# A decoder layer on one core: the attending stage with its instruction and bank orders laid out anew

## The chip, the cores and the metric

The kernel runs on one core of a Trainium2 chip. The metric is device time in microseconds (us), as the median of several runs. A core has a matmul engine (TensorE, PE in the profile; its weight loads are PEld), VectorE (DVE), ScalarE (ACT), GpSimd (POOL) and SyncE (SP), which here only issues DMAs. Each engine works through its own list of instructions in order; semaphores tie the lists together.

## The reference

For 8 sequences of 512 tokens and 512 features, in f32, three blocks follow one another, each with a residual and a layer norm behind it:

```python
x = _layernorm(x + _L0_attn_ref(x, w_qkv, w_out))        # Fourier mixing, a cumulative sum over tokens
x = _layernorm(x + _L0_xattn_ref(x, ctx, ctx, mask, ...)) # 16 heads, 77 keys for each sequence
x = _layernorm(x + _L0_ffn_ref(x, kernel, bias, a, b))    # one matmul with a quantised weight plus LoRA, bias
```

The second block is q = x W_q + b_q, masked softmax(q k^T / sqrt(32)) v for each head, then W_o and b_o. The third has a single 512 x 512 weight once quantised kernel and LoRA product are added up.

## The kernel before

Three parts run one after the other: `prepare` (weights, keys, values), `mix_tokens` (the first block for all 8 sequences, whose result x1 goes to DRAM), and `attend` (the second and third block), which the change is about. A number that is an f32 is split in two, a high part (a copy to f32r) and a low part (the difference), and each product is made of three matmuls (`split_matmuls`, L85).

`attend` is a software pipeline over i. Step i does three things for three different sequences: the front (scores, softmax and transposed probabilities of sequence i), the back (weighted values, W_o, norm, feed-forward and norm of sequence i-1) and the next (the query projection of sequence i+1). Step 0 has no back, step 7 (the closing step) no next, and step 8 (the tail) only a back. Steps 1 to 6 have the same order (the loop, `step(i)` on each engine). The order of every engine's instructions is written out by hand, one call after another.

The pieces, with the engine that does each, tiles t of 128 tokens, halves h of the heads, chunks c, groups g:

- PE: `score(i,t,h)` fills half h of score_ps; `turn_probs(i,t,c)` transposes probabilities (uses P00 to P32 of a bank, L1158); `weigh_values(g)` (V0 to V3); `project_o(t)` (O0 to O3); `turn_x2(t)` transposes the normalised tile (T0 to T3, L1191); `project_f(t)` (F0 to F3); `project_q(c)` (Q0 to Q3).
- DVE: `softmax_top(t,h)` is a masking copy (L1678) and a maximum (L1683); `invert_totals(t)` a reciprocal (L1690); `split_...` the low part of what PE left in a bank (L1634, L1643, L1662), which frees the bank; `add_o`, `add_f` add the residual and free the bank (L1702); `measure(use)` is bn_stats, bn_aggr and a small add (L1708 to L1713); `normalize_o`, `normalize_f` apply mean and rstd (L1724); `turn_x1` transposes the next x1 in blocks (L1639).
- ACT: `exponentials(t,h)` are 8 exponentials with their sums (L1357); `split_...` the high parts.
- POOL: `normalize_probs(t,h)` multiplies half a tile's probabilities with the reciprocals (L1505); `root(use)` is (var + eps)^-0.5 of 128 x 1 (L1498); `bias_residual(t)`, `bias_x2(t)` add biases (L1512, L1528); `rem_x1(c)` is the low part of the next x1 (L1519).
- SP: for each step the load of x1 for i+1 in swapped blocks, its mask, the values of i, the keys of i+1, the residual of i, and the four stores of i-1 in between, each of which waits for its `normalize_f`.

All of PE's uses but the scores share a ring of four PSUM banks. The use at place n of `BANK_ORDER` (in the first, closing and last step `START_ORDER`, `CLOSING_ORDER`, `END_ORDER`) takes bank n mod 4 and waits until the use at n-4 is freed:

```python
    def reusable(self, use):
        return self.before + (self.order.index(use) + 1 - RING)
```

`freed` is one counter, so DVE must free the banks in that same order: the order of the banks ties PE's and DVE's lists together. Other waits that matter here: `turn_probs(i,t,0)` waits for both `normalize_probs` of tile t; `turn_x2(t)` for `normalize_o(t)`; `project_f(t)` for both halves of the split of turn_x2(t); `score(i,t,h)` for the exponentials of (t-1,h); `invert_totals(t)` for the exponentials of both halves of t; `split_q(c)`, `split_o(g)` and the like on DVE for ACT's high part.

Of the kernel before, what the change touches and what calls it, by code (L numbers as in the profile page):

```python
# [463 lines left out]
def mix_tokens(nc, x, x1_dram, k_dram, mask_dram, ident, sigma, w_spec, w_back, half_power, w_q_dram, w_q, bias_q, hand):  # L464
# [4 lines left out]
    with ExitStack() as ctx:  # L469
# [296 lines left out]
        def _(dve):  # L766
# [124 lines left out]
            def split_q(c):  # L891
# [25 lines left out]
BANK_ORDER = ["V0", "V1", "V2", "V3", "O0", "O1", "T0", "O2", "F0", "P00", "P01", "T1", "P02", "O3",  # L917
              "F1", "T2", "P10", "P11", "P12", "F2", "Q0", "Q1", "P20", "T3", "Q2", "P21", "P22", "F3",
# [61 lines left out]
def attend(nc, ins, out, x1_dram, k_dram, v_dram, ffn_dram, ident, half_power, w_q, bias_q, bias_v, bias_o, bias_f,  # L980
# [3 lines left out]
    with ExitStack() as ctx:  # L984
# [140 lines left out]
        def _(pe):  # L1125
# [81 lines left out]
            def step(i):  # L1207
# [46 lines left out]
            score(0, s, 1, 1)  # L1254
            turn_probs(0, s, 0, 0)
            turn_probs(0, s, 0, 1)
            score(0, s, 2, 0)
# [7 lines left out]
            project_q(1, s, 0)  # L1265
            turn_probs(0, s, 2, 0)
            project_q(1, s, 1)
            turn_probs(0, s, 2, 1)
            project_q(1, s, 2)
            turn_probs(0, s, 2, 2)  # L1270
            turn_probs(0, s, 3, 0)
            turn_probs(0, s, 3, 1)
            turn_probs(0, s, 3, 2)
# [7 lines left out]
            weigh_values(B - 2, s, 1)  # L1281
            score(B - 1, s, 1, 0)
            weigh_values(B - 2, s, 2)
            score(B - 1, s, 1, 1)
            weigh_values(B - 2, s, 3)
            score(B - 1, s, 2, 0)
# [3 lines left out]
            project_o(B - 1, s, 0)  # L1290
            project_o(B - 1, s, 1)
            score(B - 1, s, 2, 1)
            score(B - 1, s, 3, 0)
            turn_x2(B - 1, s, 0)
            project_o(B - 1, s, 2)
            turn_probs(B - 1, s, 1, 0)
            project_f(B - 1, s, 0)
            turn_probs(B - 1, s, 1, 1)
            score(B - 1, s, 3, 1)
            turn_probs(B - 1, s, 1, 2)  # L1300
# [712 lines left out]
```

## Time and profile before

| | |
|---|---|
| median of 3 runs | 946.08 us (945.35 to 946.32) |
| the profiled execution | 946.56 us, of which its span is 944.70 us |
| busy in the span | PE 890.7, PEld 729.5, DVE 675.1, ACT 378.1, POOL 414.4 us |
| attending stage | from about 465.5 us of the span to its end |

In the profile an engine is busy while an instruction of its own runs; waits on semaphores are not busy time, and a wait is put down to the engine that released it last. Ends of matmuls are modelled: they overlap, so the distance between starts is the time one takes. PEclk is the granted clock of the matmul engine as a share of 2.4 GHz.

### The profile page before, as it was taken

The page shows a single profiled execution, that of the slowest core. Times are in us where ns is not written, and L with a number is a line of the kernel's source. Part 1 is how long each engine was busy: PE and PEld are TensorE (multiplying, and loading weights), DVE is VectorE, ACT ScalarE, POOL GpSimd, SP SyncE. Part 2 cuts the span into 40 slices and gives each one's busy share as a digit, 9 for nine tenths or more (in the row PEclk, how much of TensorE's full clock was granted, in tenths as well). Part 3 has the DMA queues.
Part 4 walks back from the last instruction along what each step waited for, and adds up shares of the span by engine and source line. Part 5 has one row for each costly group of instructions (what it writes and reads, how often), then busy time and mean ns, then how long its engine had stood idle before and what let it go on. Part 6 is the DMA issues. An engine that isn't in the chain of part 4 may idle for free. (4 is left out here: it accounts for less than half of the span.)

```text
span 944.7 us, 14374 instructions
## 1 busy us (share of the span) xinstructions
PE 890.7 (94%) x4220; PEld 729.5 (77%) x4220; DVE 675.1 (71%) x1136; ACT 378.1 (40%) x1403; POOL 414.4 (44%) x366
## 2 busy tenths in 40 slices
PE   4897999999999999999779999999999999999995
PEld 4783787888888888887667888888888888888774
DVE  2364456666666676656776988888888888888957
ACT  3262221112020202102188565756557575567610
POOL 2000364433333435323356654736547364465534
PEclk9996999999999999999969999999999999999999
DMA  5965450416133320205354024151331514112021
GB/s 183 316 168 87 92 89 23 112 37 97 52 83 69 64 89 0 90 14 128 83 135 105 14 81 88 26 132 25 99 53 24 135 31 116 27 43 70 15 79 44
DMA packets 195994, 76.02 MB, mean 80 GB/s; under 512 B 170407, under 2 KB 172711, under 8 KB 195951
## 3 DMA queue, kind: packets, MB, share of 16 engines
q1 hardware_dynamic: 195951, 75.49, 32.9%
q8 instruction: 21, 0.34, 0.1%
q14 instruction: 22, 0.18, 0.1%
HBM read 52.60 MB, written 22.87 MB: 80 GB/s over the span
## 5 line engine op out<-in xcount | busy, mean ns | idle before, releaser
L1357 ACT ACTIVATE probs<-score_ps,top_s 128x77 f32<-128x77 f32 x512 | 158.8, 358 | 32.4 <-DVE top_s L1683 24.6
L1505 POOL TENSOR_TENSOR probs<-probs,per_total 128x616 f32<-128x616 f32 x64 | 84.8, 1329 | 95.7 <-DVE per_total L1690 95.2
L1357 ACT ACTIVATION_READ_ACCUMULATOR probs<-score_ps,top_s 128x1 f32 x512 | 121.7, 240 | 0.0
L703 POOL TENSOR_TENSOR xT_lo<-x_tok,xT_hi 128x512 fp32r<-128x512 f32 x28 | 37.9, 1358 | 76.9 <-ACT xT_hi L653 76.9
L719 POOL TENSOR_TENSOR vals<-qs_prod 128x512 f32<-128x512 f32 x32 | 41.0, 1293 | 69.4 <-DVE qs_prod L814 69.4
L710 POOL TENSOR_TENSOR mix_rstd<-mix_ve,half_power 128x1 f32<-128x1 f32 x32 | 22.0, 689 | 112.7 <-DVE mix_ve L833 112.6
L666 ACT ACTIVATE qT_hi<-vals 128x512 fp32r<-128x512 f32 x32 | 19.4, 631 | 122.2 <-POOL vals L719 106.4
L1498 POOL TENSOR_TENSOR rstd<-ve,half_power 128x1 f32<-128x1 f32 x64 | 37.9, 591 | 68.8 <-DVE ve L1713 68.6
L1364 ACT ACTIVATE pT_hi<-shared_ps 103x512 fp32r<-103x512 f32 (+1 forms) x96 | 53.5, 608 | 35.9 <-PE shared_ps L1158 35.8
L1678 DVE COPY_PREDICATED score_ps<-hidden,masked 128x616 f32<-128x616 int32 x64 | 58.4, 912 | 9.3 <-PE score_ps L85 8.6
L659 ACT ACTIVATE v_sb<-v_ps 128x512 f32<-128x512 f32 x32 | 18.9, 594 | 114.5 <-PE v_ps L85 114.5
L1662 DVE TENSOR_TENSOR pT_lo<-shared_ps,pT_hi 103x512 fp32r<-103x512 f32 (+1 forms) x96 | 62.6, 680 | 0.0
L85 PE MATMUL v_ps<-xT_hi,w_spec_hi 128*128 128x512 f32 x128 | 51.8, 405 | 6.6 <-DVE xT_lo L776 6.6
L1158 PE MATMUL shared_ps<-ident,probs 128*103 128x128 f32 (+1 forms) x384 | 54.5, 283 | 2.7 <-POOL probs L1505 2.7
L1512 POOL TENSOR_TENSOR x_tok<-x_tok,bias_o 128x512 f32<-128x512 f32 x32 | 46.0, 1458 | 21.4 <-DMA x_tok<-x_between 21.2
L85 PE MATMUL shared_ps<-w_o_hi,xT_hi 128*128 128x512 f32 x128 | 52.8, 413 | 2.0 <-DVE xT_lo L1643 1.8
L1158 PEld LDWEIGHTS shared_ps<-ident,probs 128*103 128x103 f32 (+1 forms) x384 | 47.9, 162 | 8.2 <-POOL probs L1505 3.4
L1683 DVE TENSOR_REDUCE top_s<-score_ps 128x8 f32<-128x616 f32 x64 | 51.2, 800 | 3.6
L85 PE MATMUL shared_ps<-w_ffn_hi,xT_hi 128*128 128x512 f32 x120 | 48.8, 407 | 4.6 <-DVE xT_lo L1634 2.9
L1519 POOL TENSOR_TENSOR xT_lo<-x,xT_hi 128x512 fp32r<-128x512 f32 x28 | 41.8, 1515 | 24.8 <-ACT xT_hi L1340 24.8
L786 DVE TENSOR_TENSOR kv_prod<-k_ps,v_sb 128x512 f32<-128x512 f32 x16 | 11.0, 685 | 57.7 <-PE k_ps L85 57.7
L85 PE MATMUL score_ps<-xT_hi,qT_hi 128*128 128x308 f32 x128 | 42.7, 334 | 9.7 <-ACT probs L1357 7.7
(205 smaller groups left out, 2723.6 us busy)
## 6 DMA issues: line engine op xcount, KB each, us to landing
x_tok<-in_x SPq DMA_DIRECT2D x32, 256.0 KB, 4.6
x_res<-in_x SPq DMA_DIRECT2D x8, 1024.0 KB, 7.0
x_between<-mix_x SPq DMA_DIRECT2D x32, 256.0 KB, 2.0
x<-x_between SPq DMA_DIRECT2D x32, 256.0 KB, 4.1
x_tok<-x_between SPq DMA_DIRECT2D x8, 1024.0 KB, 5.8
out<-y_out SPq DMA_DIRECT2D x32, 256.0 KB, 2.2
wqkv_sb<-in_w_qkv SPq DMA_DIRECT2D x4, 768.0 KB, 7.6
keys_split<-w_q_hi SPq DMA_DIRECT2D x8, 154.0 KB, 5.8
```

The costliest lines, as they stand in the source:

```text
L85: last = nc.tensor.matmul(out, l, r, start=(n == 0), stop=(n == len(terms) - 1))
L703: nc.gpsimd.tensor_tensor(xT[half][1][:, c, :], x_tok[half][:, c, :], xT[half][0][:, c, :].bitcast(F32), ALU.subtract).then_inc(x_lo, 1)
L719: nc.gpsimd.tensor_tensor(vals[:, h, :], qs[:, 2 * h, :], qs[:, 2 * h + 1, :], ALU.subtract if h else ALU.add).then_inc(vals_summed, 1)
L1158: last = nc.tensor.transpose(shared_ps[s.bank(use)][0:size, g * P:(g + 1) * P], probs[:, t % 2, g * GK + at:g * GK + at + size], ident[:])
L1357: nc.scalar.activation(probs[:, t % 2, j * KEYS:(j + 1) * KEYS], score_ps[:, g, k * KEYS:(k + 1) * KEYS], ACT.Exp, bias=top[:, t % 2, j:j ...
L1364: nc.scalar.activation(pT[0][0:size, c, :, t * P:(t + 1) * P], turned_bank(s, t, c), ACT.Copy).then_inc(turned_hi, 1)
L1505: nc.gpsimd.tensor_tensor(p, p, per_total[:, t % 2, h * heads:(h + 1) * heads].unsqueeze(2) .to_broadcast([P, heads, KEYS]), ALU.mult).the ...
L1512: nc.gpsimd.tensor_tensor(res1[:, t, :], res1[:, t, :], bias_o[:], ALU.add).then_inc(res1_ready, 1)
L1519: nc.gpsimd.tensor_tensor(x1T[1][:, c, :], x1[:, c, :], x1T[0][:, c, :].bitcast(F32), ALU.subtract).then_inc(x1T_lo, 1)
L1662: nc.vector.tensor_tensor(pT[1][0:size, c, :, tok], turned_bank(s, t, c), pT[0][0:size, c, :, tok].bitcast(F32), ALU.subtract).then_inc(fr ...
L1678: nc.vector.copy_predicated(s4, hidden[:, t, :].unsqueeze(1).unsqueeze(1).to_broadcast(shape), masked[:].unsqueeze(1).unsqueeze(1).to_broa ...
L1683: nc.vector.tensor_reduce(top[:, t % 2, h * 8:(h + 1) * 8].rearrange("p (g j) -> p g j", j=GH), s4, AX.X, ALU.max, negate=True).then_inc(t ...
```

## The change

No instruction is added, removed or altered, and no wait has another condition. Only places change: in the bank orders of the loop, first and closing step, and in the lists of PE, ACT, POOL and DVE for the loop, the first step, the closing step and (POOL and DVE only) the tail. `END_ORDER`, PE's and ACT's lists of the tail and SP's list stay. The core of the diff:

```diff
-BANK_ORDER = ["V0", "V1", "V2", "V3", "O0", "O1", "T0", "O2", "F0", "P00", "P01", "T1", "P02", "O3",
-              "F1", "T2", "P10", "P11", "P12", "F2", "Q0", "Q1", "P20", "T3", "Q2", "P21", "P22", "F3",
+BANK_ORDER = ["V0", "V1", "V2", "V3", "O0", "O1", "P00", "P01", "T0", "O2", "F0", "T1", "P02", "O3",
+              "F1", "T2", "P10", "P11", "P12", "F2", "Q0", "T3", "Q1", "P20", "Q2", "P21", "P22", "F3",
               "P30", "P31", "P32", "Q3"]
-START_ORDER = ["P00", "P01", "P02", "P10", "P11", "P12", "Q0", "P20", "Q1", "P21", "Q2", "P22", "P30",
-               "P31", "P32", "Q3"]
-CLOSING_ORDER = ["V0", "V1", "V2", "V3", "P00", "P01", "P02", "O0", "O1", "T0", "O2", "P10", "F0",
-                 "P11", "P12", "T1", "O3", "F1", "P20", "T2", "P21", "P22", "F2", "T3", "P30", "P31",
+START_ORDER = ["P00", "P01", "P02", "P10", "P11", "P12", "Q0", "Q1", "P20", "P21", "P22", "P30", "P31",
+               "Q2", "P32", "Q3"]
+CLOSING_ORDER = ["V0", "V1", "V2", "V3", "O0", "P00", "P01", "P02", "O1", "T0", "O2", "P10", "P11",
+                 "F0", "T1", "P12", "O3", "F1", "T2", "P20", "P21", "P22", "F2", "T3", "P30", "P31",
                  "P32", "F3"]
```

PE's list in the loop step:

```diff
                 score(i, s, 2, 0)
+                turn_probs(i, s, 0, 0)
+                turn_probs(i, s, 0, 1)
                 turn_x2(i, s, 0)
                 project_o(i, s, 2)
                 project_f(i, s, 0)
-                turn_probs(i, s, 0, 0)
-                turn_probs(i, s, 0, 1)
                 score(i, s, 2, 1)
...
                 turn_probs(i, s, 1, 0)
+                turn_probs(i, s, 1, 1)
                 score(i, s, 3, 1)
-                turn_probs(i, s, 1, 1)
                 turn_probs(i, s, 1, 2)
                 project_f(i, s, 2)
                 project_q(i + 1, s, 0)
+                turn_x2(i, s, 3)
                 project_q(i + 1, s, 1)
                 turn_probs(i, s, 2, 0)
-                turn_x2(i, s, 3)
```

The loop step's lists on POOL and DVE, as they are after the change, up to the parts that the prediction steps through:

```python
# POOL
bias_residual(0), bias_residual(1), normalize_probs(0,0), normalize_probs(0,1), root O0, root O1,
bias_residual(2), bias_x2(0), normalize_probs(1,0), bias_residual(3), normalize_probs(1,1), bias_x2(1),
root O2, root F0, rem_x1(0..3), root O3, normalize_probs(2,0), bias_x2(2), normalize_probs(2,1), ...
# DVE
softmax_top(0,0), split_o(0), softmax_top(0,1), split_o(1..3), softmax_top(1,0), softmax_top(1,1),
invert_totals(0), add_o(0), turn_x1(0), measure O0, add_o(1), normalize_o(0), measure O1,
split_probs(0,0), split_probs(0,1), split_x2(0), softmax_top(2,0), invert_totals(1), turn_x1(1),
add_o(2), normalize_o(1), measure O2, softmax_top(2,1), add_f(0), split_x2(1), measure F0, ...,
normalize_o(3), measure F1, softmax_top(3,1), add_f(2), split_q(0), measure F2, normalize_f(1),
invert_totals(3), ..., normalize_f(2), split_q(3), normalize_f(3)
```

Before, POOL had root O0 between the two products of tile 0 and root O1 behind bias_x2(0); DVE had invert_totals(0) ahead of softmax_top(1,1), softmax_top(2,1) behind split_x2(1), and softmax_top(3,1) ahead of normalize_o(3).

The first step, where ScalarE and VectorE now do the last half of the softmax ahead of the query splits:

```diff
             exponentials(0, 3, 0)
+            exponentials(0, 3, 1)
             split_q(1, s, 0)
+            split_q(1, s, 1)
             split_probs(0, s, 2, 0)
-            exponentials(0, 3, 1)
-            split_q(1, s, 1)
```

The tail on DVE:

```diff
             measure(B, s, "O0")
+            add_o(B, s, 1)
             normalize_o(B, s, 0)
-            add_o(B, s, 1)
             measure(B, s, "O1")
+            add_o(B, s, 2)
             normalize_o(B, s, 1)
-            add_o(B, s, 2)
+            split_x2(B, s, 0)
             measure(B, s, "O2")
-            split_x2(B, s, 0)
             add_o(B, s, 3)
...
             measure(B, s, "F0")
+            split_x2(B, s, 2)
             normalize_o(B, s, 3)
             normalize_f(B, s, 0)
-            split_x2(B, s, 2)
```

On POOL the tail now has bias_residual(0), (1), (2), root O0, bias_residual(3), bias_x2(0), root O1, bias_x2(1), root O2; before, bias_residual(2) stood behind root O0 and bias_residual(3) behind root O1.

## Rows read from the trace of the kernel before

**Rows 1.** Windows by stage: length, busy us (instructions) of each engine, granted clock, DMA.
```profile
465.50:508.70 43.20, 30.81 (x145) 26.98 (x146) 31.82 (x47) 34.03 (x150) 22.46 (x16) 0.80 0.41 93
...
565.60:851.45 285.85, 282.40 (x1461) 237.63 (x1460) 245.14 (x446) 178.19 (x780) 157.74 (x140) 1.00 0.30 69
851.45:895.77 44.32, 42.56 (x233) 35.95 (x232) 38.20 (x68) 30.96 (x149) 25.60 (x21) 1.00 0.13 38
895.77:944.70 48.93, 37.74 (x160) 29.54 (x160) 32.00 (x64) 5.74 (x10) 17.57 (x19) 0.96 0.17 59
```

**Rows 2.** Chain of waits in a loop step (i = 5): start, us, what.
```profile
753.82 0.71 DVE x L1639
...
754.63 1.34 DVE x_and_res L1724
...
762.28 0.87 PE shared_ps L1158 x8
```

**Rows 3.** Timeline of PE, same step: start, us, instruction, [idle before, releaser].
```profile
755.14 0.30 PE L85 MATMUL score_ps<-xT_lo,qT_hi 128*128 128x308 f32 x1
756.09 0.65 PE L1191 MATMUL shared_ps<-ident,x_and_res 128*128 128x128 f32 x4 [0.65 <-DVE x_and_res L1724]
...
767.88 0.40 PE L85 MATMUL shared_ps<-w_ffn_hi,xT_hi 128*128 128x512 f32 x1
```

**Rows 4.** Timeline of POOL, same step.
```profile
750.63 1.59 POOL L1505 TENSOR_TENSOR probs<-probs,per_total 128x616 f32<-128x616 f32 x1 [6.87 <-DVE per_total L1690]
753.95 0.55 POOL L1498 TENSOR_TENSOR rstd<-ve,half_power 128x1 f32<-128x1 f32 x1 [1.73 <-DVE ve L1713]
754.46 1.22 POOL L1505 TENSOR_TENSOR probs<-probs,per_total 128x616 f32<-128x616 f32 x1
```

**Rows 5.** Timeline of DVE, same step.
```profile
749.50 0.80 DVE L1683 TENSOR_REDUCE top_s<-score_ps 128x8 f32<-128x616 f32 x1
750.22 0.24 DVE L1690 RECIPROCAL per_total<-total 128x16 f32<-128x16 f32 x1
...
758.27 0.67 DVE L1708 BATCH_NORM_STATS2 stats<-y 128x6 f32<-128x512 f32 x1
...
759.56 0.84 DVE L1678 COPY_PREDICATED score_ps<-hidden,masked 128x616 f32<-128x616 int32 x1
...
761.84 0.54 DVE L1724 TENSOR_SCALAR x_and_res<-y,mv,rstd 128x512 f32<-128x512 f32 x1
...
766.60 0.68 DVE L1634 TENSOR_TENSOR xT_lo<-shared_ps,xT_hi 128x512 fp32r<-128x512 f32 x1
```

**Rows 6.** Groups by line and shape, 565.6 to 851.45: busy us, mean ns, idle before.
```profile
L1678 DVE COPY_PREDICATED score_ps<-hidden,masked 128x616 f32<-128x616 int32 x40 | 35.1, 878 | 4.0 <-PE score_ps L85 3.6
```

**Rows 7.** Timeline of SP's DMA queue, same step.
```profile
739.23 4.75 SPq L78 DMA_DIRECT2D x<-x_between  x4
```

**Rows 8.** Timeline of PE in the first step.
```profile
504.50 0.68 PE L1158 MATMUL shared_ps<-ident,probs 128*103 128x128 f32 x4 [1.41 <-POOL probs L1505]
```

**Rows 9.** Timeline of DVE in the first step.
```profile
501.19 0.24 DVE L1690 RECIPROCAL per_total<-total 128x16 f32<-128x16 f32 x1
```

**Rows 10.** Timeline of PE in the closing step and the tail.
```profile
889.84 0.47 PE L85 MATMUL shared_ps<-w_ffn_hi,xT_hi 128*128 128x512 f32 x1 [0.70 <-DVE xT_lo L1634]
893.61 0.66 PE L1191 MATMUL shared_ps<-ident,x_and_res 128*128 128x128 f32 x4 [0.74 <-DVE x_and_res L1724]
...
924.80 0.47 PE L85 MATMUL shared_ps<-w_ffn_hi,xT_hi 128*128 128x512 f32 x1 [2.00 <-DVE xT_lo L1634]
...
932.96 0.47 PE L85 MATMUL shared_ps<-w_ffn_hi,xT_hi 128*128 128x512 f32 x1 [1.47 <-ACT qT_hi L1376]
```

**Rows 11.** Timeline of DVE in the tail.
```profile
920.68 1.41 DVE L1724 TENSOR_SCALAR x_and_res<-y,mv,rstd 128x512 f32<-128x512 f32 x1 [0.76 <-POOL rstd L1498]
...
923.86 0.68 DVE L1634 TENSOR_TENSOR xT_lo<-shared_ps,xT_hi 128x512 fp32r<-128x512 f32 x1
```

**Rows 12.** Window of the tail's low clock, columns as in rows 1.
```profile
908.95:913.50 4.55, 4.55 (x13) 3.59 (x14) 0.00 (x0) 0.00 (x0) 0.45 (x1) 0.62 0.01 4
```

More of the change, by code:

```diff
@@ L1272, in _ @@
             turn_probs(0, s, 3, 1)
+            project_q(1, s, 2)
             turn_probs(0, s, 3, 2)
@@ L1281, in _ @@
             weigh_values(B - 2, s, 1)
+            weigh_values(B - 2, s, 2)
+            weigh_values(B - 2, s, 3)
             score(B - 1, s, 1, 0)
-            weigh_values(B - 2, s, 2)
             score(B - 1, s, 1, 1)
-            weigh_values(B - 2, s, 3)
-            score(B - 1, s, 2, 0)
+            project_o(B - 1, s, 0)
             turn_probs(B - 1, s, 0, 0)
@@ L1400, in step @@
                 split_probs(i, s, 1, 0)
+                split_probs(i, s, 1, 1)
                 split_x1(i + 1, s, 3)
-                split_probs(i, s, 1, 1)
                 split_probs(i, s, 1, 2)
                 exponentials(i, 3, 0)
+                split_x2(i, s, 3)
+                split_q(i + 1, s, 0)
                 exponentials(i, 3, 1)
-                split_q(i + 1, s, 0)
                 split_q(i + 1, s, 1)
                 split_probs(i, s, 2, 0)
-                split_x2(i, s, 3)
                 split_q(i + 1, s, 2)
@@ L1422, in _ @@
             exponentials(0, 1, 1)
+            split_probs(0, s, 0, 0)
             split_x1(1, s, 0)
-            split_probs(0, s, 0, 0)
             split_probs(0, s, 0, 1)
+            split_probs(0, s, 0, 2)
+            exponentials(0, 2, 0)
             split_x1(1, s, 1)
-            exponentials(0, 2, 0)
-            split_probs(0, s, 0, 2)
             split_x1(1, s, 2)
@@ L1460, in _ @@
             split_o(B - 2, s, 3)
+            exponentials(B - 1, 1, 0)
             split_probs(B - 1, s, 0, 0)
@@ L1611, in _ @@
             bias_residual(B - 1, 1)
+            bias_residual(B - 1, 2)
             root(B, s, "O0")
-            bias_residual(B - 1, 2)
-            root(B, s, "O1")
             bias_residual(B - 1, 3)
             bias_x2(B, s, 0)
+            root(B, s, "O1")
+            bias_x2(B, s, 1)
             root(B, s, "O2")
             root(B, s, "O3")
-            bias_x2(B, s, 1)
+            bias_x2(B, s, 2)
             root(B, s, "F0")
-            bias_x2(B, s, 2)
+            root(B, s, "F1")
             bias_x2(B, s, 3)
-            root(B, s, "F1")
             root(B, s, "F2")
@@ L1746, in step @@
                 softmax_top(i, 1, 0)
+                softmax_top(i, 1, 1)
                 invert_totals(i, 0)
-                softmax_top(i, 1, 1)
                 add_o(i, s, 0)
+                turn_x1(i + 1, 0)
                 measure(i, s, "O0")
-                turn_x1(i + 1, 0)
+                add_o(i, s, 1)
                 normalize_o(i, s, 0)
-                turn_x1(i + 1, 1)
-                add_o(i, s, 1)
-                turn_x1(i + 1, 2)
-                split_x2(i, s, 0)
-                measure(i, s, "O1")
-                softmax_top(i, 2, 0)
+                measure(i, s, "O1")
+                split_probs(i, s, 0, 0)
+                split_probs(i, s, 0, 1)
+                split_x2(i, s, 0)
+                softmax_top(i, 2, 0)
+                invert_totals(i, 1)
+                turn_x1(i + 1, 1)
                 add_o(i, s, 2)
                 normalize_o(i, s, 1)
-                invert_totals(i, 1)
                 measure(i, s, "O2")
+                softmax_top(i, 2, 1)
                 add_f(i, s, 0)
-                split_probs(i, s, 0, 0)
-                split_probs(i, s, 0, 1)
+                split_x2(i, s, 1)
                 measure(i, s, "F0")
-                split_x2(i, s, 1)
-                softmax_top(i, 2, 1)
+                turn_x1(i + 1, 2)
                 normalize_o(i, s, 2)
@@ L1802, in step @@
                 split_probs(i, s, 3, 2)
+                normalize_f(i, s, 2)
+                split_q(i + 1, s, 3)
                 normalize_f(i, s, 3)
-                split_q(i + 1, s, 3)
             s = Shared(0, False, True, True)
@@ L1841, in _ @@
                                         ALU.subtract).then_inc(w_o_lo, 1)
-            split_probs(0, s, 3, 0)
             split_probs(0, s, 3, 1)
+            split_q(1, s, 2)
             split_probs(0, s, 3, 2)
```

187 lines of the change are left out of this document (92 added, 95 removed).

## The prediction

> **What bounds the kernel now.** I read the windows by stage first [rows 1]: in the six loop steps of the attending stage the matmul engine (PE) is busy for all but some 1% of the time, at a granted clock of 1.00; five of the steps take 285.85 us, 57.17 each. Before the loop (465.5 to 508.7), in the closing step and in the tail behind it, PE is idle for 12.4, 1.8 and 11.2 us. So in the loop only what PE waits for counts, and there is little of it; at the two ends there is more. The chain of waits [rows 2] and PE's own timeline [rows 3] then name the one real wait of a loop step: turn_x2(i,0), which transposes the first normalised tile, starts at 756.09; the score product before it issued its last matmul at 755.14 and one takes 0.14, so PE stood from 755.28, 0.81 us. It waits for normalize_o(i,0) on DVE (1.34 us in the chain), and that for the root on POOL. POOL's timeline [rows 4] shows root O0 at 753.95 squeezed between the two products normalize_probs(i,0,0) and (i,0,1); the second starts at 754.46, and the normalisation that starts 0.17 us later takes 1.34 instead of the 0.54 that the same instruction takes at 761.84 [rows 5]. PE has no other wait in a step that its timeline shows as idle time.
>
> **Loop step, the change by parts.** No instruction is added or removed; instructions only change places in their queues, so every cost is a wait that comes or goes.
>
> (a) turn_probs(i,0,0) and (i,0,1), 0.87 us of PE in the chain [rows 2], move from behind project_f(i,0) to ahead of turn_x2(i,0), into the 0.81 us wait. Are the probabilities ready? The reciprocal stood at 750.22 [rows 5], now softmax_top(i,1,1) goes ahead of it: a copy (0.84 at 759.56, 0.88 in the mean) and a reduction (0.80) [rows 5, 6], less 0.08 of overlap (749.50 + 0.80 against 750.22), put it at 751.8 or 751.9, its end at 752.0 and the first product at 752.2 by the old lag of 0.17 (750.22 + 0.24 against 750.63). POOL now runs both products before root O0: 2 x 1.22 [rows 4] gives 754.6, before PE's 755.28. Root O0 (0.55) then ends at 755.15 and the normalisation starts at about 755.25, not 754.63; but POOL now waits for the next variance, so it takes 0.54 and ends at 755.8, against 755.97 before. PE does the pair until 756.1 and finds the tile ready. Gain 0.8 us a step, if nothing later is late.
>
> (b) What is late next: DVE has no idle time from here to project_f(i,1), which PE started at 767.88 [rows 3] and would now start at 767.0. It needs split_x2(i,1), which stood at 766.60 [rows 5]. In the new order DVE does, from 755.7: measure O1 (1.2, the distance from 758.27 to 759.56 less a short wait), two split_probs, split_x2(i,0), softmax_top(i,2,0), a reciprocal, turn_x1(1), add_o(2), normalize_o(1), measure O2, softmax_top(i,2,1), add_f(0), split_x2(i,1). With 0.68 for a split or add, 1.6 for a softmax_top, 0.24, 0.71 [rows 2], 0.54 and 1.2 that is 1.2 + 1.3 + 0.7 + 1.6 + 0.2 + 0.7 + 0.7 + 0.5 + 1.2 + 1.6 + 0.7 + 0.7 = 11.1, less about 0.08 for each of twelve overlaps: 10.2. It ends at 765.9, 0.9 before LDWEIGHTS wants it (766.8). Every copy or normalisation that meets a running POOL instruction costs 0.8 (1.34 - 0.54) and there are three in that stretch; POOL is full too, with bias_residual(2), bias_x2(0), normalize_probs(1,0), bias_residual(3) and (1,1) there. I count normalize_o(1) and the second copy as disturbed, partly, by 0.3 and 0.6: just at the limit, so no stall, and no further gain from the tenth-sized waits ahead of O3, F1 and F2, which together could give 0.6 more. turn_x2(i,1) needs normalize_o(1) at 762.97 in the new PE order; it ends at 762.2 to 762.5.
>
> (c) The second half of a step: softmax_top(i,3,1) moves back behind normalize_o(3) and measure F1, some 2.3 us, and with it exponentials(3,1), the last reciprocal and the two products. PE wants these only behind project_f(3); stepped through the same way they are there about 2.8 us before: hidden, and the first thing to show if that cover is gone. project_q(1) behind turn_x2(3) costs one more change of operand, 0.1.
>
> (d) Queues: SP sends store 1 and then the residual load when normalize_f(1) is done, which comes some 6 us earlier; so the residual's biases on POOL leave the place beside softmax_top(0,*). normalize_f(3) now stands behind split_q(3), so the last store, and behind it the swapped load of x1, go 1.2 us later: its issue at 739.23 takes 4.75 us [rows 7], the first turn_x1, at 753.82 in the chain [rows 2], now comes at 752.5. Issue over at 744.0 + 1.2 leaves 7 us for landing. Nothing.
>
> Six steps: 6 x 0.8 = 4.8 (bounds: 0, if (b) eats it, and 8.4 at 1.4 a step). The Trainium skill ("SBUF — State Buffer", Who interferes with whom) has it that GpSimd and such DVE instructions take the shared port pair as a lock for a whole instruction, and that who issues first wins. The trace agrees that order decides (1.34 against 0.54), but the wait it shows is 0.8, not the whole 1.22 product.
>
> **Opening (i = 0).** PE waits 1.41 us for the last products at 504.50 [rows 8], whose reciprocal ran at 501.19 [rows 9] behind exponentials(3,1), which ScalarE did behind split_q(0) and split_probs(2,0). Both now come behind it, so the reciprocal falls near 497.5 and that wait goes. Against it: the first reciprocal moves behind a softmax_top (1.1 late, but score(2,0) fills PE), turn_probs(3,0) and (3,1) now stand ahead of project_q(2) and wait for split_q(1) and split_probs(2,0) (about 0.5), and weigh_values(0) waits for the last split. Net -0.7 (0 to -1.4).
>
> **Closing step.** Two waits of PE, 0.70 and 0.74 [rows 10], bound the gain at 1.4. PE's order is close to the old one for its length; by the same stepping project_f(2) waits for split_x2(2) as before, the last reciprocal is 2.5 us later in DVE's list, and normalize_o(3) earlier. I take -0.4 (-1.4 to +1.5, two disturbances in the list).
>
> **Tail.** PE waits 2.00 us at 924.80 (project_f(0)) and 1.47 at 932.96 (project_f(2)) [rows 10]. The first is for split_x2(0), which DVE did at 923.86 [rows 11], behind add_o(2) and measure O2. Now it stands right behind normalize_o(1), which started at 920.68 and took 1.41 beside a running bias_residual on POOL [rows 11]; in the new order that bias and bias_x2(0) are over before root O1, so it takes 0.54. Even from an unmoved 920.68 the split is done at 920.68 + 0.54 + 0.68 = 921.9, and PE's idle time began at 922.80 (924.80 - 2.00): -2.0. The second goes because split_x2(2) no longer stands behind normalize_f(0), which waited and was disturbed: -1.5. Together -3.5 (-2 to -4). The low clock of the stretch after a pause of PE of some 1.8 us (0.62 from 908.95 to 913.50 [rows 12]) costs 12 matmuls some 1.6 us; the pause stays, and whether the clock falls again I leave open, at -1.6 or 0; in the sum 0.
>
> **Sum.** The profiled execution took 946.56 us (span 944.70 and 1.86 around it). 946.56 - 4.8 - 0.7 - 0.4 - 3.5 = 937.2. It was 0.48 above the median of the runs (946.08), by which the same sum gives 936.7; I forecast 937.0, a per cent faster.
>
> **Rivals.**
> 1. The lock: each meeting costs DVE the rest of the POOL instruction. The second copy starts 0.2 after a product of 1.22 and waits 1.0 instead of 0.6, so project_f(i,1) is 0.4 late in every step: 6 x 0.4 = 2.4, 939.4. Against it: the 0.8 where 1.05 was left of the product (754.46 + 1.22 - 754.63). The rule of the page named above would have it so.
> 2. (b) takes all of the loop's gain: 0.8 a step more than I count, as one more disturbed instruction would. 937.0 + 4.8 = 941.8. For it: DVE has no gap there. Against: 0.9 us of slack before disturbances.
> 3. Slower: the same queue of DVE, with all of its disturbable instructions and add_f(0) behind POOL. From a stall of 1.6 us a step on ((4.8 + 4.6) / 6, 4.6 being the other stages) it outweighs everything; at 2.4 (three meetings beyond the slack) it gives 946.6 + 6 x (2.4 - 0.8) - 4.6 = 951.6. For it: rows 4 and 5 show that one meeting costs 0.8; against it, that POOL idles until the reciprocal.
> 4. No effect: other waits of a tenth each fill what was won, and the tail's chain runs over ScalarE and POOL anyway: 946. Against it stand the 2.00 and 1.47.
> 5. More: loop steps at -1.4, opening -1.4 and the clock kept in the tail: 946.6 - 8.4 - 1.4 - 0.4 - 3.5 - 1.6 = 931.3.
>
> **Numbers.** Chances: forecast 0.50 (934 to 938.5), lock 0.15, rival 2 0.14, more 0.09, slower 0.07, no effect 0.05. The range 932.5 to 943.5 leaves out the last two and about half of "more". Within 0.2% (1.9 us) a measurement of this kernel can't be told from no change: faster 0.87, same 0.06, slower 0.07.
>
> **What the profile after would show.** Right: loop steps of about 56.4 us in the chain; no wait ahead of turn_x2(i,0), the normalisation there at 0.54; project_f(i,1) without idle time before it; no 1.41 before the last probabilities of the opening; project_f(0) of the tail right behind its transposes. Wrong: PE waiting for xT_lo (L1634) once a step, copies (L1678) with a mean above 0.88, or a low clock in a new place of the opening or the tail.

## The result and the profile after

| | before | after |
|---|---|---|
| median of the timed runs, us | 945.74 | 947.61 |
| ratio after / before (95% interval) | | 1.0016 (1.0009 to 1.0023) |
| profiled execution: span, us | 944.70 | 946.5 |
| loop, from the scores of step 1 to those of the last step | 342.77 | 348.74 |
| behind it, to the end of the span | 93.09 | 89.16 |

The kernel got slightly slower, by 0.16%, where 937.0 us, a per cent less, was forecast. Not every part failed: what lies behind the loop got 3.93 us shorter, 3.9 was forecast (closing step and tail together). The opening gave 0.24 instead of 0.7. The loop was to lose 4.8 us and gained 5.97, one us a step.

The windows by stage of the kernel after, columns as in [rows 1] (opening's end, five loop steps, closing step, tail):

```profile
465.50:508.60 43.10, 30.84 (x146) 26.63 (x147) 32.70 (x47) 33.64 (x149) 22.12 (x16) 0.76 0.41 94
566.67:857.34 290.67, 282.52 (x1462) 237.24 (x1462) 251.91 (x446) 177.51 (x780) 166.50 (x141) 1.00 0.29 68
857.34:901.90 44.56, 42.41 (x233) 36.15 (x233) 38.77 (x71) 30.78 (x148) 23.32 (x20) 1.00 0.10 26
901.90:946.50 44.60, 36.87 (x161) 29.31 (x159) 28.39 (x61) 5.96 (x10) 17.67 (x19) 0.95 0.19 65
```

PE did the same work in the loop (282.52 us busy, 282.40 before), at the same full clock, but the five steps take 290.67 instead of 285.85 us. DVE is busy 251.91 instead of 245.14 us with the same 446 instructions, 1.35 us a step, and POOL 166.50 instead of 157.74. Instructions that only changed places got longer.

PE's waits between 509 and 850 us: sum in us, number of times, longest. Before, this view has one row, for the tile of [rows 3]; it is gone, and two others stand there:

```profile
PE shared_ps L85 <- DVE xT_lo L1634: 7.3, 12, 0.7
PE shared_ps L1158 <- DVE y L1702: 2.2, 6, 0.4
```

In PE's timeline of one loop step (i = 4; its scores start at 682.96, those of the next step at 741.04) the old wait's place and the new waits are:

```profile
700.97 1.03 PE L1158 MATMUL shared_ps<-ident,probs 128*103 128x128 f32 x8
701.84 0.60 PE L1191 MATMUL shared_ps<-ident,x_and_res 128*128 128x128 f32 x4
...
713.15 0.50 PE L85 MATMUL shared_ps<-w_ffn_hi,xT_hi 128*128 128x512 f32 x1 [0.69 <-DVE xT_lo L1634]
...
720.24 0.47 PE L85 MATMUL shared_ps<-w_ffn_hi,xT_hi 128*128 128x512 f32 x1 [0.57 <-DVE xT_lo L1634]
...
729.61 0.68 PE L1158 MATMUL shared_ps<-ident,probs 128*103 128x128 f32 x4 [0.36 <-DVE y L1702]
```

The pair of transposes runs ahead of turn_x2(i,0), and that starts without a wait, as part (a) had it. Then project_f(i,1) waits 0.69, project_f(i,2) 0.57 and turn_probs(i,2,0) 0.36 us, all for DVE.

DVE's timeline of the same step shows why. A copy usually takes 0.80 us and a normalisation 0.54; these are the ones that took clearly longer, with the first normalisation (undisturbed), the statistics behind it and one split:

```profile
700.93 0.54 DVE L1724 TENSOR_SCALAR x_and_res<-y,mv,rstd 128x512 f32<-128x512 f32 x1
701.39 0.69 DVE L1708 BATCH_NORM_STATS2 stats<-y 128x6 f32<-128x512 f32 x1
...
709.22 1.66 DVE L1678 COPY_PREDICATED score_ps<-hidden,masked 128x616 f32<-128x616 int32 x1 [0.20 <-issue]
...
712.23 0.68 DVE L1634 TENSOR_TENSOR xT_lo<-shared_ps,xT_hi 128x512 fp32r<-128x512 f32 x1
...
714.57 1.62 DVE L1724 TENSOR_SCALAR x_and_res<-y,mv,rstd 128x512 f32<-128x512 f32 x1
...
717.32 0.76 DVE L1724 TENSOR_SCALAR y_out<-y,mv,rstd 128x512 f32<-128x512 f32 x1
...
726.35 1.77 DVE L1678 COPY_PREDICATED score_ps<-hidden,masked 128x616 f32<-128x616 int32 x1
```

And POOL's timeline beside them:

```profile
709.00 1.21 POOL L1505 TENSOR_TENSOR probs<-probs,per_total 128x616 f32<-128x616 f32 x1
...
714.11 0.55 POOL L1498 TENSOR_TENSOR rstd<-ve,half_power 128x1 f32<-128x1 f32 x1 [1.58 <-DVE ve L1713]
714.63 1.29 POOL L1519 TENSOR_TENSOR xT_lo<-x,xT_hi 128x512 fp32r<-128x512 f32 x1
...
726.25 1.21 POOL L1505 TENSOR_TENSOR probs<-probs,per_total 128x616 f32<-128x616 f32 x1
```

I call it a meeting when such an instruction of DVE runs beside a long one of POOL and takes longer for it. There are three large meetings a step: the copy of softmax_top(2,1) with normalize_probs(1,1) (0.86 us too long), normalize_o(2) with the first remainder of x1 (1.08), the copy of softmax_top(3,1) with normalize_probs(2,1) (0.97), 2.9 us in all. Two small ones, of normalize_o(1) (0.05) and normalize_f(0) (0.22, at 717.32), make it 3.1 or 3.2. The first normalisation, which met a product before, is undisturbed. The groups by line and shape over the five steps say it as means: the copies took 878 ns before [rows 6], and now

```profile
L1678 DVE COPY_PREDICATED score_ps<-hidden,masked 128x616 f32<-128x616 int32 x40 | 40.9, 1023 | 1.7 <-issue 1.2
L1724 DVE TENSOR_SCALAR x_and_res<-y,mv,rstd 128x512 f32<-128x512 f32 x20 | 16.5, 823 | 0.0
```

The chain of waits, which ran over PE in most of a step before, now runs over DVE from 700.33 to 729.61; some of its lines, the last three being PE's again:

```profile
709.22 1.67 DVE score_ps L1678
...
714.57 1.62 DVE x_and_res L1724
...
726.35 1.78 DVE score_ps L1678
...
728.87 0.69 DVE y L1702
729.61 0.68 PE shared_ps L1158 x4
730.29 3.00 PE shared_ps L85 x12
```

### The profile page after: what moved, and what is told of

Same layout as the page of the kernel before. It is cut to its first block, busy times and chain, and to the rows that moved or that the text cites. A ratio compares the mean times of both kernels' runs of the same rounds, so it can differ in the third digit from the quotient of the medians.

```text
span 946.5 us, 14374 instructions
## 1 busy us (share of the span) xinstructions
PE 889.5 (94%) x4220; PEld 728.2 (77%) x4220; DVE 682.2 (72%) x1136; ACT 377.8 (40%) x1403; POOL 423.3 (45%) x366
## 4 chain that ended last, share of the span: by engine, by line
PE 25%; DVE 16%; issue 6%; ACT 2%; POOL 1%; DVEq 1%; POOLq 0%
PE shared_ps L85 20%; DVE score_ps L1678 4%; PE score_ps L85 3%; DVE stats L1708 2%; DVE y L1702 2%; PE shared_ps L1158 2%; ACT probs L1357 2%; DVE x_and_res L1724 2%; DVE pT_lo L1662 1%; DVE xT_lo L1634 1%; DVE x L1639 1%; DVE mv L1711 1%; DVE y_out L1724 1%; DVE top_s L1683 1%; POOL probs L1505 0%
## 5 line engine op out<-in xcount | busy, mean ns | idle before, releaser
L1505 POOL TENSOR_TENSOR probs<-probs,per_total 128x616 f32<-128x616 f32 x64 | 87.9, 1386 | 121.4 <-DVE per_total L1690 120.8
L1678 DVE COPY_PREDICATED score_ps<-hidden,masked 128x616 f32<-128x616 int32 x64 | 66.5, 1039 | 6.6 <-PE score_ps L85 4.4
L1498 POOL TENSOR_TENSOR rstd<-ve,half_power 128x1 f32<-128x1 f32 x64 | 40.4, 631 | 63.8 <-DVE ve L1713 63.7
L1528 POOL TENSOR_TENSOR x_and_res<-x_and_res,bias_f 128x512 f32<-128x512 f32 x32 | 53.1, 1660 | 5.0 <-DVE x_and_res L1724 3.8
L85 PE MATMUL v_ps<-xT_hi,w_spec_lo 128*128 128x512 f32 x128 | 51.5, 403 | 0.0
```

Source lines behind the costliest of these rows:

```text
L85: last = nc.tensor.matmul(out, l, r, start=(n == 0), stop=(n == len(terms) - 1))
L1498: nc.gpsimd.tensor_tensor(rstd[:, n:n + 1], ve[:, n:n + 1], half_power[:], ALU.pow).then_inc(rstd_ready, 1)
L1505: nc.gpsimd.tensor_tensor(p, p, per_total[:, t % 2, h * heads:(h + 1) * heads].unsqueeze(2) .to_broadcast([P, heads, KEYS]), ALU.mult).the ...
L1528: nc.gpsimd.tensor_tensor(res2[:, t % 2, :], x2[:, t % 2, :], bias_f[:], ALU.add).then_inc(res2_ready, 1)
L1678: nc.vector.copy_predicated(s4, hidden[:, t, :].unsqueeze(1).unsqueeze(1).to_broadcast(shape), masked[:].unsqueeze(1).unsqueeze(1).to_broa ...
```

## The experiments

Two theories stood at first. **Meetings**: DVE waits for no other engine from 701 to 736 us, so every meeting with POOL goes into the step's length. **Order**: DVE's and PE's new orders cost by themselves, and the longer instructions fall where there is room. Step lengths below are distances between the scores of two steps in the chain or between the same product on POOL. The quiet kernels, softmax_top(2,1) back in its place, the two biases quiet and the first of the two kernels with the biases first were executed once each; the other times are medians of 5 to 12 executions.

### Old loop, new ends

The kernel before with the new START_ORDER and CLOSING_ORDER, and with the new lists of the first and the closing step and of the tail; the loop stays old.

```diff
-START_ORDER = ["P00", "P01", "P02", "P10", "P11", "P12", "Q0", "P20", "Q1", ...
+START_ORDER = ["P00", "P01", "P02", "P10", "P11", "P12", "Q0", "Q1", "P20", ...
...
 # DVE's tail (POOL's too)
+                add_o(B, s, 2)
                 normalize_o(B, s, 1)
-                add_o(B, s, 2)
+                split_x2(B, s, 0)
                 measure(B, s, "O2")
-                split_x2(B, s, 0)
```

> The loop step as before, the first step, closing step and tail as after the change. Both theories put the whole loss into the loop (+5.97 us over its six steps) and the gain elsewhere (-3.9 behind the loop, -0.24 ahead of it), so about 945.7 - 4.1 = 941.6 us, ratio 0.9956. If stages depend on each other (the phase in which the loop hands over to the closing step), some of the 3.9 is missing: 943 or more.

Measured: 940.95 us, ratio 0.9942 (0.9925 to 0.9959), steps of 57.1. The ends are worth 4 to 5 us; the loop alone eats them.

### Both kernels with a quiet POOL

The long POOL instructions of the attending stage (products of the softmax, both biases, remainders of x1) work on one element of each row instead of all; their number, order and waits stay, and the values that they leave out are missing from the output. Once with the kernel after, once with the kernel before.

```diff
-nc.gpsimd.tensor_tensor(res1[:, t, :], res1[:, t, :], bias_o[:], ALU.add)
+nc.gpsimd.tensor_tensor(res1[:, t, 0:1], res1[:, t, 0:1], bias_o[:, 0:1], ALU.add)
```

> The kernel after, with POOL's products, biases and x1 remainders in the attending stage on 1 element of each row instead of hundreds (so these values are wrong); nothing moved. Theory M (meetings: DVE instructions that find POOL at work are blocked for 0.9 to 1.1 us, three times a step, on a DVE list without idle time): copies (L1678) at 0.80 all over, DVE busy per step from 50.4 to about 47.5, PE's waits ahead of project_f(1), project_f(2) and turn_probs(2,0) gone or under 0.2, loop step 58.1 -> 56.3 to 56.6. Theory O (places: two softmax_tops stand ahead of what PE needs): the step stays above 57.4.

> The same on the kernel before. Theory M: its own meetings cost DVE 1.4 us a step, of which PE feels only the 0.8 ahead of turn_x2(0); step 57.17 -> 56.4 to 56.6, so no longer than that of quiet_after (the new order is no worse once nothing meets). Theory O: 56.4, and quiet_after stays 1 us above it.

Measured: after 927.45 us, steps of 55.51 (58.13 with the meetings); before 931.53, steps of 55.87 (57.17). With no meetings PE's timeline marks no wait in the loop of either kernel, and the copies take their 0.80. The group of the copies in the quiet kernel after:

```profile
L1678 DVE COPY_PREDICATED score_ps<-hidden,masked 128x616 f32<-128x616 int32 x42 | 33.8, 804 | 2.1 <-issue 1.2 <-PE score_ps L85 0.4
```

POOL's work costs the kernel after 2.6 us a step and the kernel before 1.3. Without it the new order is 0.36 us a step faster, so the order by itself isn't the cause; what it wins is less than what POOL's work takes from it. That this work costs by the meetings, and not because POOL's own results come late, the runs below have to show.

### softmax_top(2,1) back in its old place

The kernel after, DVE's loop list:

```diff
                 measure(i, s, "O2")
-                softmax_top(i, 2, 1)
                 add_f(i, s, 0)
                 split_x2(i, s, 1)
+                softmax_top(i, 2, 1)
```

> The kernel after, in the loop softmax_top(2,1) back behind split_x2(1) as before the change; nothing else. Theory M, by which the whole DVE list from measure O1 to the third softmax_top is the chain: the 0.69 us wait ahead of project_f(1) goes, but comes back ahead of project_f(2), step within 0.3 of 58.1 unless the copy now misses POOL (then 0.8 less). Theory O: 0.7 less, 57.4.

Measured: 948.67 us, steps of 58.10. Of the twelve waits for the split (L1634) six are left; the wait of project_f(1) is gone, and the time is the same: part of the wait stands in front of turn_x2(2) (L1191), and that of project_f(2) went from 0.57 to 0.64:

```profile
PE shared_ps L85 <- DVE xT_lo L1634: 3.8, 6, 0.6
...
PE shared_ps L1191 <- DVE x_and_res L1724: 1.0, 5, 0.2
```

So the wait where the shortage first shows isn't the cost; what counts is the length of DVE's whole list up to its next wait for another engine.

### The two biases alone quiet

The kernel after with only bias_residual (L1512) and bias_x2 (L1528) on one element; the edit is that of the quiet kernels, for these two lines.

> The kernel after with only the two bias additions of POOL (L1512, L1528) on 1 element of each row, so these biases are wrong; the products and the x1 remainders keep their length, and nothing that DVE waits for on POOL in the softmax gets shorter. quiet_after took all of POOL's long work away and with it POOL's own delays; this tells the two apart. Meetings: DVE's blocked copies and normalisations fall from three a step to one or two, step 58.1 -> 56.5 to 57.3. If the gain of quiet_after was POOL's shorter chain (products, roots) and not the meetings: still about 58.

Measured: 939.43 us, steps of 57.2. The copies are back at 808 ns, although the products that they met are still there: the one of tile 1 is over at 705.57, and the copy of softmax_top(2,1) starts at 705.67. x_and_res stays at 821 and keeps its meeting with the remainder of x1. Two of the three large meetings are gone (1.8 us), but normalize_f(0) now starts with the second remainder (712.95 and 712.96) and takes 1.57 us, 1.03 too long where it was 0.22. That is 1.0 us of meetings less, and the step is 0.9 shorter.

### The biases first

The kernel after, POOL's loop list: bias_residual(2) and (3) right behind (0) and (1). The second run has, besides, bias_x2(1) behind root O2, normalize_o(2) ahead of measure F0, and add_f(2) and split_q(0) ahead of softmax_top(3,1).

```diff
                 bias_residual(i - 1, 0)
                 bias_residual(i - 1, 1)
+                bias_residual(i - 1, 2)
+                bias_residual(i - 1, 3)
                 normalize_probs(i, 0, 0)
...
-                bias_residual(i - 1, 2)
                 bias_x2(i, s, 0)
                 normalize_probs(i, 1, 0)
-                bias_residual(i - 1, 3)
                 normalize_probs(i, 1, 1)
```

> The kernel after, in the loop bias_residual(2) and (3) moved on POOL right behind (0) and (1), where POOL idles 13.6 us; whole output computed. Meetings: normalize_probs(1,1) runs at 707.6 (in the frame of the profile after) instead of 709.0 and misses the copy of softmax_top(2,1), but bias_x2(1) behind it may take its place: step between 57.3 and 58.1. If meetings didn't matter: 58.1.

> The kernel after, its loop mended against meetings: POOL does bias_residual(2), (3) first and bias_x2(1) behind root O2; DVE does normalize_o(2) ahead of measure F0, and add_f(2) and split_q(0) ahead of softmax_top(3,1). Meetings: step 58.1 -> 56.3 to 57.0, so 947.6 - 6 x 1.1 to 1.8 = 937 to 941. If DVE's list is too full even so, it stays above 57.4 and the whole above 943.

Both missed by far: 960.78 us for the first, with steps of 60.1 that grow to 61.7, 955.3 (ratio 1.0097, 1.0079 to 1.0114) with 59.5 for the second. POOL's and DVE's timelines at the start of a step of the first:

```profile
748.15 5.52 POOL L1512 TENSOR_TENSOR x_tok<-x_tok,bias_o 128x512 f32<-128x512 f32 x4
```

```profile
750.42 0.75 DVE L1643 SCALAR_TENSOR_TENSOR qT_lo<-shared_ps,bias_q,qT_hi 128x512 fp32r<-128x512 f32 x1 [0.58 <-ACT qT_hi L1345]
751.09 1.44 DVE L1724 TENSOR_SCALAR y_out<-y,mv,rstd 128x512 f32<-128x512 f32 x1
752.45 1.89 DVE L1678 COPY_PREDICATED score_ps<-hidden,masked 128x616 f32<-128x616 int32 x1
```

POOL waits 13 us for the first reciprocal, which looked like free room for the biases. But four of them keep it busy until 753.7, across normalize_f(3), which the change put behind split_q(3), and the first copy of softmax_top: 2.0 us more of DVE. The exponentials come late, with them ScalarE's halves of split_o, and PE waits with a score product for the exponentials (0.7) and ahead of project_o(0) (1.0). Room on one engine is no room if the other's instructions stand beside it.

### One and two meetings at a time

Three kernels, all the kernel after with edits in the loop. "apart" is the second run above without the moved biases.

```diff
 # apart: POOL, then DVE
-                bias_x2(i, s, 1)
                 root(i, s, "O2")
+                bias_x2(i, s, 1)
...
+                normalize_o(i, s, 2)
                 measure(i, s, "F0")
                 turn_x1(i + 1, 2)
-                normalize_o(i, s, 2)
...
-                softmax_top(i, 3, 1)
                 add_f(i, s, 2)
                 split_q(i + 1, s, 0)
+                softmax_top(i, 3, 1)
```

> The kernel after, with three changes of place in the loop that take two of its three meetings apart: bias_x2(1) behind root O2 on POOL, normalize_o(2) ahead of measure F0, add_f(2) and split_q(0) ahead of softmax_top(3,1) on DVE. The biases stay where after has them. If DVE's list with its meetings is the bound, two meetings of 1.08 and 0.97 less are at most 2.0 us a step; the step without any meeting was 55.5 and the first meeting (0.86) stays, so 56.3 to 57.3 a step and 937 to 943 in all, x_and_res (L1724) at a mean near 550 ns. The rival, that the order of the list itself and not the meetings broke the run with all the biases ahead, has the step stay near 58 or go up, 947 or more, as the three changes of place are the same there.

Measured: 948.5 us (1.0024, 1.0011 to 1.0038), steps of 58.3, a miss. The normalisation is at 0.54 (714.11) and the third large meeting is gone too (a small one came, 0.31 us for the copy at 722.44, beside the last remainder), but DVE got two gaps for it:

```profile
728.32 0.75 DVE L1643 SCALAR_TENSOR_TENSOR qT_lo<-shared_ps,bias_q,qT_hi 128x512 fp32r<-128x512 f32 x1 [0.86 <-ACT qT_hi L1345]
728.99 0.80 DVE L1678 COPY_PREDICATED score_ps<-hidden,masked 128x616 f32<-128x616 int32 x1
...
733.33 0.25 DVE L1690 RECIPROCAL per_total<-total 128x16 f32<-128x16 f32 x1 [1.11 <-ACT probs L1357]
```

split_q(0) waits for ScalarE, and the copy queued behind it ends at 729.8 instead of 728.1, while the step itself runs 1.27 us later in this trace (first product 699.14 against 697.87): 0.4 later in the step in spite of the two meetings saved. exponentials(3,1) are late with it; PE waits 1.28 once a step, and 0.69 ahead of project_f(1) as before. My edit swapped a meeting for a wait in the queue.

"one_gone" edits POOL alone, "two_gone" has the first two pairs of lines of "apart" as well:

```diff
                 bias_residual(i - 1, 1)
+                bias_residual(i - 1, 2)
                 normalize_probs(i, 0, 0)
...
-                bias_residual(i - 1, 2)
                 bias_x2(i, s, 0)
+                bias_residual(i - 1, 3)
                 normalize_probs(i, 1, 0)
-                bias_residual(i - 1, 3)
```

> The kernel after, with POOL's loop list alone edited and nothing brought to the place of the first copies but what before has there: bias_residual(2) right behind (1), bias_residual(3) behind bias_x2(0), in POOL's wait for the second reciprocal, then both products of tile 1. The second of these then runs from about 26.1 to 27.3 of the step and no longer beside softmax_top(2,1), whose copy stands at 26.3 with 1.66 us: it may still be caught by its tail, so 0.5 to 0.9 us of DVE less. If the meetings are the cost, the wait of project_f(1) (0.69) shrinks or goes and the step is 57.3 to 57.8: 942 to 945.5. If the order of DVE's list is the cost, 58.15 stays: 947.6.

> one_gone, and bias_x2(1) behind root O2 on POOL with normalize_o(2) ahead of measure F0 on DVE (the second meeting, 1.08 us; in the last run the normalisation took 0.54 there). split_q(0) stays behind softmax_top(3,1), so that the copy doesn't wait for ScalarE. Meetings as the cost: up to 0.9 + 1.1 us a step less than after, the third meeting (0.97) stays: 56.2 to 57.1, 936 to 941.5 in all. Order as the cost: 947.6 or more.

Measured: one_gone 951.46 us (1.0059, 1.0045 to 1.0073), steps of 59.0, a miss. No meeting went: bias_x2(1) moved up into the copy's way, and the third bias at the step's start meets normalize_f(3) (0.91 us), after which PE waits 0.81 ahead of project_o(0). DVE's timeline, and POOL's instruction beside its second row:

```profile
686.34 1.45 DVE L1724 TENSOR_SCALAR y_out<-y,mv,rstd 128x512 f32<-128x512 f32 x1
...
712.05 1.65 DVE L1678 COPY_PREDICATED score_ps<-hidden,masked 128x616 f32<-128x616 int32 x1 [0.20 <-issue]
```

```profile
711.76 1.27 POOL L1528 TENSOR_TENSOR x_and_res<-x_and_res,bias_f 128x512 f32<-128x512 f32 x1
```

two_gone: 941.61 us (0.9957, 0.9944 to 0.9971), steps of 57.2 (one of 57.5), just above the bracket for meetings and far from 947.6. It differs from one_gone by two swaps that take both middle meetings away, and is 1.8 us a step faster; the new meeting at the start stays and is what the bracket left out.

The kernels with the new loop side by side. The meetings are what DVE's copies took above 0.80 us and its normalisations above 0.54, read from the timelines as a mean of four steps; the step is the mean of the same four.

| kernel | meetings, us a step | step, us |
|---|---|---|
| quiet after | 0.0 | 55.6 |
| two biases quiet | 2.2 | 57.2 |
| two_gone | 2.3 | 57.3 |
| softmax_top(2,1) back | 3.0 | 58.1 |
| after | 3.1 | 58.1 |
| one_gone | 4.0 | 59.0 |
| apart | 1.2 | 58.3 |
| biases first, second run | 2.4 | 59.5 |
| biases first, first run | 5.1 | 61.3 |

From two biases quiet to one_gone the step grows with the meetings nearly one for one, 1.7 us for 1.8, whether POOL's instructions were shortened or, as in one_gone and two_gone, only moved. POOL's results coming late isn't the cause: in the loop of the kernel after neither DVE nor PE has a single wait for POOL. The last three lie above that line, and each has waits that the others lack: for ScalarE in DVE's list, or of PE at the step's start.

### The old wait, taken away on POOL alone

The kernel before, and the kernel with the new ends of the first experiment, each with this edit of POOL's loop list:

```diff
                 bias_residual(i - 1, 2)
+                bias_residual(i - 1, 3)
                 normalize_probs(i, 0, 0)
-                root(i, s, "O0")
                 normalize_probs(i, 0, 1)
-                bias_residual(i - 1, 3)
-                bias_x2(i, s, 0)
+                root(i, s, "O0")
                 root(i, s, "O1")
+                bias_x2(i, s, 0)
```

> The ends kernel (loop of before, the rest of after) with one edit in POOL's loop list: both products of tile 0 and bias_residual(3) ahead of root O0, root O1 behind it, so that POOL stands waiting while DVE normalises O0. Meetings: that normalisation takes 0.54 instead of 1.34, PE's 0.81 wait ahead of turn_x2(0) goes, step 57.17 -> 56.4 to 56.8 if project_f(1) does not wait; 940.95 - 2.2 to -4.6 = 936.4 to 938.8. If the slack of split_x2(1) is gone: 940.

> The kernel before, with POOL's loop list alone edited: both products of tile 0 and bias_residual(3) ahead of root O0, root O1 right behind it. In the run with the new ends this took the step from 57.15 to 56.39, 0.76. If stages add up: the same 0.76 x 6 = 4.6 here, 945.7 - 4.6 = 941.1 (940 to 942.5), the step at 56.4. If the gain of the run before was bound to the new first step (a different phase of the engines carried into the loop), less: 943 to 946.

Measured: on the kernel before 941.07 us (0.9942, 0.9923 to 0.996), steps of 56.40; with the new ends 935.6 (0.9888, 0.9871 to 0.9905), steps of 56.4. That is faster than both kernels. The group of the normalisation in the latter:

```profile
L1724 DVE TENSOR_SCALAR x_and_res<-y,mv,rstd 128x512 f32<-128x512 f32 x20 | 10.9, 543 | 5.5 <-POOL rstd L1498 5.0
```

Four biases stand at the head of POOL's list here too, and harm nothing. POOL's timeline of the kernel with the new ends, whose step starts some 3 us before this row:

```profile
680.96 5.60 POOL L1512 TENSOR_TENSOR x_tok<-x_tok,bias_o 128x512 f32<-128x512 f32 x4 [4.34 <-DMA x_tok<-x_between]
```

In the old loop, as this row shows, the residual's load holds them back, past normalize_f(3) (678.27) and the first copy (679.58), to where DVE has gaps; it is issued 3.5 us ahead of the step's first scores (674.40 and 677.93). The new loop issues it 8.3 us ahead (732.74 and 741.04 in the kernel after), and the biases start in the middle of DVE's work. By these traces that is why the same move helped here and hurt there; no run changes the time of the load alone.

The step lost 0.77 us, the wait of [rows 3]; the copies stay at 879 ns, and PE's timeline marks no wait in the loop. PE's and DVE's old orders had room (this group now idles 5.5 us in five steps), so little came back later.

## Why the prediction failed where it did

**(a) was right.** The pair of transposes fills the wait, both products are done, and the normalisation at 700.93 takes 0.54 us.

**(b) was mis-sized by 0.4 us.** From measure O1 to the end of split_x2(1) DVE took 11.5 us (701.39 to 712.91). The disturbances there are 0.86 for the copy and 0.05 for normalize_o(1), 0.9 as in the forecast. The work between them is 10.6 us, not 10.2: I took 0.08 off at each of twelve joints, and the trace has gaps of 0.15 to 0.2 ahead of each aggregation and of the copy. PE, too, is there earlier than forecast: from the end of the scores (700.97) to where it wants project_f(1) (712.30) it needs 11.3 us, where the forecast has 11.7 (755.28 to 767.0). The stretch was forecast to fit exactly; 0.4 and 0.4 make the 0.85 that pass from 712.30 to 713.15, of which the timeline marks 0.69 as the wait.

**(c) is the step that failed: "hidden".** I looked only at whether softmax_top(3,1) is in time, and priced no meeting in the second half of the step, though DVE waits for no other engine there either. normalize_o(2) and the copy of softmax_top(3,1) met POOL for 1.08 and 0.97 us. project_f(2) waits 0.57 for its split, and turn_probs(2,0) waits 0.36 for the bank that add_f(2), behind that copy, frees.

**What the three waits cost.** The marks of the timeline sum to 1.62 us. By the distance between starts, as the prediction measured its 0.81, they cost more. Around project_f(1), in the kernel after:

```profile
712.07 0.39 PE L85 MATMUL shared_ps<-w_o_lo,xT_hi 128*128 128x512 f32 x1
...
713.48 0.40 PE L85 MATMUL shared_ps<-w_ffn_hi,xT_lo 128*128 128x512 f32 x1
```

From the first of these matmuls to the other it is 1.41 us; in the quiet kernel after, where the same two start at 701.90 and 702.38, it is 0.48. Around project_f(2) it is 1.48 (719.07 to 720.55) against 0.67 (707.96 to 708.63), around turn_probs(2,0) 1.74 (728.86 to 730.60) against 0.90 (716.90 to 717.80). The three differences are 2.58 us, of the 2.62 by which the two steps differ: nothing else makes the kernel after slower than its quiet twin. The step forecast (56.4) lies 0.9 above the quiet one (55.5), so 2.6 us of waits gave 58.1, 1.8 over the forecast. Rival 3 had this mechanism, with a chance of 0.07; its 951.6 put 2.4 us on top of 56.4 instead of 55.5. Its argument "one meeting costs 0.8" held, and I hadn't laid POOL's new list beside DVE's over the whole step to count them.

**Rival 1, the lock's price.** The copy waited 0.86 us where 0.99 were left of the product, nearer to the rule than the 0.6 I took; here it changed nothing, as normalize_o(1) cost 0.05 instead of 0.3.

**(d)** was right in that none of PE's waits in the attending stage, before or after, is for a transfer. The residual's load comes 4.6 us earlier in the step (8.3 us ahead of the scores instead of 3.7), not 6. It cost nothing in the kernel after, with two biases at the step's start; it let the third and fourth bias that some runs put there run beside normalize_f(3) and the first copy.

**Opening: mis-sized.** It gave 0.24 us of the 0.7. The score product that was to fill PE while the first reciprocal runs later waits itself: 2.02 us at 479.65, for the exponentials, where before PE waited 1.33 for the first products (478.91). Behind it a copy meets the next products (483.10, 1.70 us instead of 0.80). At the end of the opening the wait for the last products fell from 1.41 to 0.75 us, and another of 0.23 came ahead of it:

```profile
500.12 0.64 PE L1158 MATMUL shared_ps<-ident,probs 128*102 128x128 f32 x4 [0.23 <-DVE qT_lo L1643]
501.51 1.12 PE L1158 MATMUL shared_ps<-ident,probs 128*103 128x128 f32 x8 [0.75 <-POOL probs L1505]
```

**Closing step and tail: right in sum.** The closing step took 44.56 us (44.32 before): three waits, of 0.67, 1.00 and 0.41, took the place of the old 0.70 and 0.74 [rows 10], so +0.2 instead of -0.4. The tail lost 4.3, more than the forecast 3.5 (the windows' edges are good to some 0.2; by the chain the two lost 3.9): from 919 us on PE's timeline shows no wait, and both of [rows 10] are gone. The low clock stayed: PE pauses 1.77 us ahead of project_o(0), and from 915 to 917 us the granted clock is 0.50, the level of 1.2 GHz. The eight matmuls from 914.76 on take 3.48 us instead of 1.84 at the distance of 0.23 that they have at full clock, so the 1.6 us that the prediction read from [rows 12] are lost here too.

```profile
874.06 0.41 PE L85 MATMUL score_ps<-xT_hi,qT_hi 128*128 128x308 f32 x1 [0.67 <-ACT probs L1357]
...
896.50 0.47 PE L85 MATMUL shared_ps<-w_ffn_hi,xT_hi 128*128 128x512 f32 x1 [1.00 <-DVE xT_lo L1634]
900.39 1.56 PE L1158 MATMUL shared_ps<-ident,probs 128*103 128x128 f32 x12 [0.41 <-POOL probs L1505]
...
914.76 0.69 PE L85 MATMUL shared_ps<-w_o_hi,xT_hi 128*128 128x512 f32 x1 [1.77 <-DVE xT_lo L1643]
```

**Left open.** A version that keeps the new loop, computes everything and has none of the meetings wasn't found. How much of the length of the last three kernels of the table comes from each of their waits, no run takes apart.

## What to carry to other kernels

When an engine's list leaves it no wait for another engine, moving one instruction of it changes its phase against the other engine for the rest of the step: lay both new lists side by side over the whole step, and price every pair that can meet, not only up to the first wait. A wait moved away from PE isn't won until the engine behind it has slack; topping up one place moved the wait and left the time. Look first for the edit that takes the disturbance away at its source: here the places of a few instructions on POOL gave nearly the whole gain forecast for the loop (4.6 of 4.8 us), while a loop laid out anew on four engines lost 6 us. The edit on POOL together with the new ends gave 935.6 us, less than the 937.0 forecast for the whole change.

## What the runs showed of the hardware

**What a meeting costs.** A copy that starts during a POOL product ends 0.66 or 0.67 us after it (710.88 against 710.21, 728.12 against 727.46), though alone it takes 0.80; a normalisation ends 0.27 to 0.29 after POOL's instruction (716.19 against 715.92; before, 755.97 against 755.68 [rows 4, 2]), alone 0.54. So in these rows the price is the rest of POOL's instruction less 0.13 or 0.26 us. The small meetings fit: in two_gone a copy that starts at 717.37 beside a remainder that ends at 717.81 ends at 718.48, 0.67 later. The Trainium skill ("SBUF — State Buffer", Who interferes with whom) has an exclusive lock for the whole instruction; by these rows that is right but for this overlap.

**Who wins.** Recorded starts don't settle it when they are close. In the kernel after, normalize_o(2) starts at 714.57, during a root (one element, 0.55 us), and POOL's remainder 0.06 us later; the normalisation waits through the whole of it. In two_gone the copy starts at 706.32, also during a root, 0.39 us ahead of bias_x2(1); it takes 0.81, and POOL's addition takes 1.55 instead of about 1.28:

```profile
706.32 0.81 DVE L1678 COPY_PREDICATED score_ps<-hidden,masked 128x616 f32<-128x616 int32 x1 [0.20 <-issue]
```

```profile
706.20 0.55 POOL L1498 TENSOR_TENSOR rstd<-ve,half_power 128x1 f32<-128x1 f32 x1
706.71 1.55 POOL L1528 TENSOR_TENSOR x_and_res<-x_and_res,bias_f 128x512 f32<-128x512 f32 x1
```

In both cases the root itself blocks nothing long; in the first, what POOL starts behind it does. POOL loses in some meetings, so it grew as well: bias_x2 (L1528) took 1.77 us in the mean in the loop after, 1.29 before.
